# An audio tower on one core: the first layer norm's two products as fp32r pairs, the experts a round later, new orders

## What is computed

```python
# tok: a window of 8 positions, weights filt * W
out = jnp.einsum('blfd,fd,fdk->blk', windows, filt, W)
h = jax.nn.relu(out + b_k)
# attention on layernorm(h), one head, softmax over the positions of one sequence
h = h + attn(layernorm(h))
# experts on layernorm(h): 8 of them, hidden width 128, the two best by gate with softmax weights
h1 = jax.nn.relu(jnp.einsum('td,edh->teh', x_flat, W1) + b1)
y = jnp.einsum('teh,ehd->ted', h1, W2) + b2
h = h + jnp.einsum('ted,te->td', y, combine)
```

## Time and profile before

| | us |
|---|---|
| median of 3 runs | 298.57 (297.52 to 299.38) |
| profiled execution, its own time | 298.85 |
| its span | 297.1 |
| PE busy | 279.3 (94%) |
| DVE busy | 241.1 (81%) |
| ACT busy | 238.9 (80%) |
| POOL busy | 103.8 (35%) |

### The profile page before, as it was taken

One profiled execution on the slowest core, in us unless ns is written; L12 is line 12 of the kernel. 1 busy time (PEld: TensorE's weight loads), 2 busy tenths in 40 slices (PEclk: granted clock), 3 DMA queues, 4 the chain that ended last, 5 costly groups with the idle time before them and its releaser, 6 DMA issues.

```text
span 297.1 us, 6188 instructions
## 1 busy us (share of the span) xinstructions
PE 279.3 (94%) x1737; PEld 200.4 (67%) x1737; DVE 241.1 (81%) x890; ACT 238.9 (80%) x549; POOL 103.8 (35%) x99
## 2 busy tenths in 40 slices
PE   7776999999999999999999999999998999998993
PEld 6544657777777768677777777686776675665572
DVE  2576669989897979889898979798898899895666
ACT  3449598898998889898989989898887788876762
POOL 2204023442536162443415351715342151506051
PEclk9998899999999999999999999999999999999999
DMA  6430206061433526170624426250605133242301
GB/s 189 108 96 9 73 34 176 4 172 57 114 113 76 152 71 158 37 191 4 164 65 109 118 71 159 71 155 31 163 2 130 45 104 89 87 105 69 91 19 34
DMA packets 12785, 27.58 MB, mean 93 GB/s; under 512 B 3152, under 2 KB 5456, under 8 KB 12752
## 3 DMA queue, kind: packets, MB, share of 16 engines
q1 hardware_dynamic: 12464, 26.91, 33.8%
q10 hardware_dynamic: 288, 0.28, 0.3%
HBM read 20.85 MB, written 2.27 MB: 78 GB/s over the span
## 4 chain that ended last, share of the span: by engine, by line
PE 69%; DVE 12%; DMA 7%; issue 5%; ACT 4%; POOL 1%; POOLq 0%; SPq 0%; DVEq 0%; ACTq 0%
PE bank_y L1379 15%; PE bank_a L1290 11%; PE bank_h L1363 7%; PE bank_h L1364 7%; PE bank_s L1307 5%; PE bank_s L1419 4%; DMA kk<-kk 4%; PE bank_s L1318 4%; PE bank_s L1386 3%; DVE acc L820 3%; PE bank_b L1390 2%; PE bank_s L1390 2%; PE bank_s L1440 2%; PE bank_b L1386 2%; PE bank_b L1430 1%
## 5 line engine op out<-in xcount | busy, mean ns | idle before, releaser
L465 ACT ACTIVATE hid<-bank_h,col 128x496 f32<-128x496 f32 x128 | 84.3, 672 | 10.8 <-PE bank_h L1364 7.1
L374 POOL TENSOR_TENSOR p<-p,rmask 124x496 f32<-124x496 f32 x32 | 32.5, 1016 | 97.9 <-DVE rmask L863 97.7
L1379 PE MATMUL bank_y<-hid,w_sb 128*64 128x248 f32 x508 | 63.7, 380 | 0.8 <-DVE acc L820 0.7
L1363 PE MATMUL bank_h<-xs,w_hi 128*128 128x496 f32 x128 | 58.1, 454 | 0.2 <-DVE xs L256 0.2
L820 DVE SCALAR_TENSOR_TENSOR acc<-bank_y,col,cb 128x248 f32<-128x248 f32 x127 | 53.1, 468 | 4.7 <-PE bank_y L1379 1.9
L1364 PE MATMUL bank_h<-xs,w_lo 128*128 128x496 f32 x128 | 49.5, 387 | 0.0
L1379 PEld LDWEIGHTS bank_y<-hid,w_sb 128*64 128x64 f32 x508 | 32.8, 136 | 24.7 <-issue 11.2
L268 POOL TENSOR_TENSOR total<-acc 128x496 f32<-128x496 f32 x16 | 20.0, 1251 | 46.1 <-DVE acc L820 45.9
L456 ACT ACTIVATE p<-bank_s,nmax 124x248 f32<-124x248 f32 x64 | 29.3, 464 | 2.3 <-DVE nmax L852 1.1
L388 POOL TENSOR_TENSOR x_lo<-x,x_hi 128x512 fp32r<-128x512 f32 x16 | 20.6, 1291 | 24.9 <-ACT x_hi L524 24.9
L1363 PEld LDWEIGHTS bank_h<-xs,w_hi 128*128 128x128 f32 x128 | 24.1, 189 | 7.0 <-issue 3.6
(11 more groups left out here) (120 smaller groups left out, 545.8 us busy)
## 6 DMA issues: line engine op xcount, KB each, us to landing
cb<-weights SPq DMA_DIRECT2D x60, 248.0 KB, 3.9
kk<-kk SPq DMA_DIRECT2D x16, 248.0 KB, 3.0
x<-xt SPq DMA_DIRECT2D x15, 256.0 KB, 3.5
out<-h SPq DMA_DIRECT2D x16, 124.0 KB, 3.7
w_sb<-w SPq DMA_DIRECT2D x3, 256.0 KB, 4.0
wtok_sb<-wtok SPq DMA_DIRECT2D x1, 256.0 KB, 2.7
x<-xt ACTq DMA_DIRECT2D x1, 256.0 KB, 3.8
weights<-ct_sb SPq DMA_DIRECT2D x15, 15.5 KB, 1.4
```

Of the source, the lines that this page charges most:

```text
L374: pool.tensor_tensor(p_sb[b][0:HALF, :, :], p_sb[b][0:HALF, :, :], rmask[0:HALF, b, :].unsqueeze(2).to_broadcast([HALF, 2, WIN]), ALU.mult ...
L465: act.activation(hid[2 * (p % 2) + s][:, :], bank_h[s][:, 0:TOK], ACT.Relu, bias=col[:, C_B1 + e:C_B1 + e + 1]).then_inc(hid_ready[s], 1)
L1363: pe.matmul(bank_h[e % 2][:, 0:TOK], w1_hi[:, e, :], xs[m % 2][:, :], start=True, stop=False)
L1379: last = pe.matmul(dst[b * D:b * D + D, :], w2_sb[:, 2 * p + s, :], hid[2 * (p % 2) + s][:, b * WIN:(b + 1) * WIN], start=True, stop=True)
```

## The change

- **Products.** From group 3 (`SPLIT_FROM`, the fourth) on, the first centring and the first variance are two fp32r products each, of a high and a low part, in place of one fp32 product. Their matrices are cast once into `center_r` and `mean_r` (DVE, in `expert_low`).
- **Parts.** ACT's `rectify` writes the high part of h, by a Relu with an fp32r result. POOL gets four instructions a group: h in full (`full_h`), its low part (`low_h`), the high part of the squares (`high_square`), their low part (`low_square`).
- **Experts.** They lag one round more behind the rest of the group, with eight `hid` buffers for four. The loop runs for t = 4 to 11.
- **Orders.** All the order functions of all engines are written anew.

```diff
-        hid = [sb(f"hid{i}", [128, TOK]) for i in range(4)]
+        hid = [sb(f"hid{i}", [128, TOK]) for i in range(EXPERTS)]
...
-        LOOP_FROM, LOOP_TO = 3, 13
+        LOOP_FROM, LOOP_TO = 4, 12
+        SPLIT_FROM = 3
...
+            def full_h(d):
+                pool.wait_ge(hsum_ready, d + 1)
+                pool.wait_ge(h2_ready, d - 1)
+                pool.tensor_scalar(h[d % 2][:, :], hsum[:, :], 0.0, None, ALU.max).then_inc(h_ready, 1)
+
+            def low_h(d):
+                pool.wait_ge(h_ready, d + 1)
+                pool.wait_ge(hh_ready, d - SPLIT_FROM + 1)
+                pool.wait_ge(cen[0], d)
+                pool.tensor_tensor(h_lo[:, :], h[d % 2][:, :], h_hi[:, :].bitcast(F32),
+                                   ALU.subtract).then_inc(hl_ready, 1)
+
+            def high_square(d):
+                pool.wait_ge(sqr[0], d + 1)
+                pool.wait_ge(var[0], d)
+                pool.tensor_copy(s_hi[:, :], sq[0][:, :]).then_inc(sh_ready, 1)
+
+            def low_square(d):
+                pool.wait_ge(sh_ready, d - SPLIT_FROM + 1)
+                pool.tensor_tensor(s_lo[:, :], sq[0][:, :], s_hi[:, :].bitcast(F32),
+                                   ALU.subtract).then_inc(sl_ready, 1)
...
-                after(act, y_done, 4 * m + p - 1)
-                act.activation(hid[2 * (p % 2) + s][:, :], bank_h[s][:, 0:TOK], ACT.Relu,
+                after(act, y_done, 4 * m + p - 3)
+                act.activation(hid[e][:, :], bank_h[s][:, 0:TOK], ACT.Relu,
...
             def square(g, which, src):
                 act.wait_ge(cen[which], g + 1)
-                after(act, var[which], g)
+                if which == 0 and g > SPLIT_FROM:
+                    act.wait_ge(sl_ready, g - SPLIT_FROM)
+                else:
+                    after(act, var[which], g)
...
+                    act.wait_ge(cen[0], d)
+                    act.activation(h_hi[:, :], hsum[:, :], ACT.Relu).then_inc(hh_ready, 1)
...
             def expert_low():
+                dve.wait_ge(par_const, 16)
+                dve.tensor_copy(center_r[:, :], center).then_inc(set_norm, 1)
+                dve.tensor_copy(mean_r[:, :], meanof).then_inc(set_norm, 1)
...
             def fill():
+                expert_high()
                 both_taps(0)
                 attention_parameters()
...
             def variance(g, which, dst):
+                if which == 0 and g >= SPLIT_FROM:
+                    pe.wait_ge(sl_ready, g - SPLIT_FROM + 1)
+                    pe.matmul(dst[:, WIN:2 * WIN], mean_r[:, :], s_hi[:, :], start=True, stop=False)
+                    pe.matmul(dst[:, WIN:2 * WIN], mean_r[:, :], s_lo[:, :], start=False,
+                              stop=True).then_inc(var[0], 1)
+                    return
...
+                pe.wait_ge(set_norm, 2)
+                pe.wait_ge(hl_ready, c - SPLIT_FROM + 1)
+                pe.matmul(bank_b[:, 0:WIN], center_r[:, :], h_hi[:, :], start=True, stop=False)
+                pe.matmul(bank_b[:, 0:WIN], center_r[:, :], h_lo[:, :], start=False, stop=True).then_inc(cen[0], 1)
```

More of the change, by code:

```diff
@@ L1217, in drain @@
[L1217 to L1232 removed]
+                difference(14)
@@ L1504, in fill @@
+                variance(2, 0, bank_b)
+                scores(1, 1)
                 conv(3, range(8, 10))
+                turn_p(1, 0)
+                turn_p(1, 1)
                 conv(3, range(10, 12))
                 turn_weights(0)
-            def iteration(t):
-                a, d, c, n, m = t + 1, t, t - 1, t - 2, t - 3
+                attend(1)
+                queries_keys(2)
+                values(2)
+                second_centre(1)
+                hidden(0, 0)
+                conv(4, range(0, 2))
@@ new lines, in fill @@
+                variance(1, 1, bank_s[0])
+                conv(4, range(2, 4))
+                conv(4, range(4, 6))
+                hidden(0, 1)
+                conv(4, range(6, 8))
+                first_centre(3)
+                gate(1)
+                hidden(0, 2)
+                hidden(0, 3)
+                scores(2, 0)
+                scores(2, 1)
+                hidden(0, 4)
+                conv(4, range(8, 10))
+                hidden(0, 5)
+                variance(3, 0, bank_b)
@@ L1586, in drain @@
+                hidden(11, 3)
+                scores(13, 0)
+                scores(13, 1)
+                conv(15, range(8, 10))
+                hidden(11, 4)
+                conv(15, range(10, 12))
+                hidden(11, 5)
+                variance(14, 0, bank_b)
+                expert_out(11, 0)
                 expert_out(11, 1)
-                conv(15, range(2, 4))
-                gate(12)
-                hidden(11, 5)
-                conv(15, range(4, 6))
                 hidden(11, 6)
-                scores(13, 0)
@@ L1609, in drain @@
+                expert_out(11, 2)
                 attend(13)
+                turn_weights(12)
+                expert_out(11, 3)
                 queries_keys(14)
                 second_centre(13)
+                hidden(12, 0)
+                hidden(12, 1)
+                variance(13, 1, bank_s[0])
+                values(14)
+                hidden(12, 2)
+                first_centre(15)
+                gate(13)
                 hidden(12, 3)
-                values(14)
-                variance(13, 1, bank_s[0])
+                scores(14, 0)
@@ L1635, in drain @@
-                attend(14)
-                queries_keys(15)
-                second_centre(14)
-                values(15)
-                hidden(13, 4)
-                variance(14, 1, bank_s[0])
-                hidden(13, 5)
+                scores(15, 0)
+                hidden(13, 4)
+                scores(15, 1)
+                hidden(13, 5)
+                hidden(13, 6)
+                expert_out(13, 0)
                 expert_out(13, 1)
-                hidden(13, 6)
-                gate(14)
```

982 lines of the change are left out of this document (597 added, 385 removed).

## The result

The changed kernel takes **301.25 us** (median of 6 runs, 300.71 to 303.31) against 298.36 for the kernel before (6 runs, 297.42 to 299.38): a ratio of 1.0115, 95% interval 1.009 to 1.0141. It is slower by about 1%, where I had forecast a gain: 294.8, with 0.12 for slower by over 1% and 0.36 for a change within 1%. The time lies inside my range of 288 to 301.5, at its end. The profiled execution of the changed kernel took 303.31 with a span of 301.5 and is the slowest of its six; the spans of the others are 298.9 to 300.0. So some 2 us of what its trace shows at the clock are more than typical.

What follows compares the result with a forecast made beforehand. PE was taken to set the loop's pace, with no engine full in the drain. Loop -3.9, fill -1.15, drain -0.8 and POOL's holds +2.1 gave -3.75 against 298.85, so 295.1, as median 294.8 us; 8-in-10 range 288 to 301.5.

Steps and rivals of the forecast that it cites:

- -3.9 forecast: Loop, group 1 to 11: ten turns of 15.94 us instead of 16.33, PE still setting the pace.
- The two savings of 0.19: PE, each group from 3 on: first centring and first variance each cost 0.23 instead of 0.42 us.
- the fill, -1.15 forecast: Start to group 1's second centring: the later start of hsum and the gains of the new order sum to -1.15 us.
- term for the cast, +1.9: Fill: the early cast of w1 waits for its loads, so DVE reaches hsum at 11.4 instead of 9.58.
- The other terms, -1.1, -1.8, -0.6 and +0.45: Fill: convolution pair moved behind -1.1, expert outputs a round later -1.8, index search moved -0.6, values before second centring +0.45.
- so it takes them in: Tail: 23.1 us for about 12 of PE work absorbs the later experts' 2.6 us, so 0 counted.
- the split's terms there: Drain and tail: half of PE's savings counted, -0.8; POOL's added instructions holding DVE, +2.1.
- the +1.3 that I had for drain and tail: Group 11 to the end: -0.8 from PE's savings and +2.1 from POOL's holds of DVE, together +1.3 us.
- My sign of being wrong: Drain: the forecast is wrong above all if the 16.17 us between groups moves by more than 0.5 either way.
- The fourth rival: Loop and drain: POOL's instructions hold DVE until it sets the pace past 0.76 us a group; 299.8 to 307.1, chance 0.15.
- Rivals 1 to 3: Drain gains, 288.0, chance 0.17; loop turn stays 16.3, 298.7, chance 0.17; fill only longer, 297.9, chance 0.08.
- rival 1: Drain: new order lets it run at DVE's 14.7 us a group, four groups saving 5.9; 288.0 us, chance 0.17.

Runs made afterwards that it cites:

- e3: Changed kernel with the split undone (single fp32 products, POOL's four instructions gone), new orders and later experts kept: 307.10 us.
- e1: Changed kernel with only the cast of w1 moved back behind the low keys of group 0: 298.29 us.
- e11: Changed kernel with POOL waiting for the early cast of w1 before the low inputs of group 1: 300.01 us.
- e2: Changed kernel with 16 dummy products in PE's idle stretch between the convolutions of groups 0 and 1, cast still early: 299.85 us.
- e5: e1 with 22 dummy products on PE in two waits of the fill, around the first turns of groups 0 and 1: 295.68 us.
- e10: Kernel before with 10 dummy products on PE in the wait for group 0's scaled scores: 297.15 us.
- e7: Kernel before with POOL's four instructions added at e4's places, writing to tiles nobody reads, products left fp32: 309.10 us.
- e6: e5 with two first expert layers of group 0 in place of the dummies around group 1's turn: 295.64 us.
- e12: e5 with 16 more products, the high product of each first expert layer of groups 14 and 15 done twice: 298.26 us.
- e13: Kernel before with 16 more products, the high product of each first expert layer of groups 14 and 15 done twice: 301.10 us.
- e14: e5 with the split for groups 3 to 11 only, single fp32 products again for 12 to 15: 296.17 us.
- e4: Kernel before with only the split, for groups 4 to 15, in the old orders and without the experts' lag: 311.73 us.
- e9: Kernel before without the 16 products with the low part of w1 for groups 14 and 15: 296.78 us.
- e8: e1 without the 16 products with the low part of w1 for groups 14 and 15: 297.36 us.

## Why the prediction was wrong

**Loop: right in the turn, too many turns.** -3.9 forecast; the turn came to 15.89 for 15.94. The two savings of 0.19 are there. Two things I had not counted cancel: a stall of 0.17 ahead of the scores (DVE's `mask`, held by POOL in e3) that went too, and 0.14 that the new orders cost (e3). The ten turns gave -2.1 in the profiled run and -2.7 in e1, since the last two already follow the drain's orders and are longer.

**The failed step: the fill, -1.15 forecast, +5.4 in the profiled run.** Its term for the cast, +1.9, cost 3.0 us of the program's time (e1 against the changed kernel). The wait for the load was sized rightly (10.7). Missing were the hold of 1.0 by POOL's instruction beside the cast (e11: 1.2 us of the time), which I had looked for in the loop and the drain only, and PE's clock, which falls in an idle time of 4.1 us and stays low behind it (e2: 1.4). The three overlap: 1.9, 1.2 and 1.4 are more than the 3.0 they cost together, for e11's edit raises the clock too, and e1's fill loses to the clock in other places. The other terms, -1.1, -1.8, -0.6 and +0.45, sum to -3.05. At full clock they gave -0.7 at most (e5 against e10; -0.2 against e7), and with the clock that this order gets, +1.2 (e1 against before). I had counted the expert outputs that leave the fill as time won. They stood mostly in waits, and the work there had kept PE's clock up, so far as the runs tell (e6 shows it for two first layers): e1 has 0.66 in 40 to 50 us, and 2.6 us came back when dummies stood there and in the gap before.

The Trainium skill (TensorE: Matmul & The Clock Gate, "Part 1: The HAM clock gate") gives the two levels that these windows show and says that activity releases the lower one; the windows of e1 and e5 agree. It puts the penalty of the ramp at under 1% of a typical kernel's span. The falls here are others, in the middle of the fill, and no ramp of the start: e5 against e1 is 0.9% and e2 against the changed kernel 0.5%.

**The second failed step: "so it takes them in", 0 for the tail.** I set 23.1 us against "about 12" of PE work and so forgot the four `spread_last`, 3.7 us by their rows; 15.5 before and 18.1 after is right. The tail grew by 4.2 and the drain shrank by 3.1, because the last groups' experts moved from one to the other; together +1.1, or nearer 2 against a typical before. At the second centring of group 11 the changed kernel has three expert layers and two outputs more still to do than before, 3 x 0.45 + 2 x 0.91 = 3.2 us that the fill no longer does. Work added near the end cost 0.7 to 0.8 of itself (e12, e13), so by my estimate that is +2.4; no run takes this work out of the end to show it. That the split's terms there were 0.8 gained and 2.1 lost, 1.3 lost in all, is not borne out either: e14 gives 0.5 gained at most. So the +1.3 that I had for drain and tail came near the measured +1.1 to +2 by luck, for other reasons than mine. My sign of being wrong did come true: the drain's distance moved from 16.17 to 15.4.

**The fourth rival** (0.15) ends near where the time ended, but not by its mechanism: in the changed kernel DVE's busy time in a turn rose by 0.13 us. Its rule was off in one point as well. I took DVE's idle time in a turn, 0.76 us beyond the attention product's wait, for slack; what counts is the way from the attention product over `lg` to the scores, and there the old kernel has none (PE already waits 0.1 us: `lg` ends at 148.89, the scores start at 149.03). e4 and e7 show that the mechanism was there for the taking, 1.1 us a turn, and that the new orders and the lag, which by themselves cost, are what keeps it off: 13.4 us more with the split in the old orders, 5.85 less with it in the new. The rows point to the places of the instructions: `kmask`, `mask` and the last sum take 0.36, 0.16 and 0.41 us in the changed kernel, 0.82, 0.64 and 0.83 in e7. What the round of slack adds was not tried. Rivals 1 to 3 did not occur as told; the drain alone came half way to rival 1.

**Open:** why two runs of one kernel differ in the fill's clock (the changed kernel's six spans go with clocks of 0.967 to 0.983). Not every low stretch costs time: e12's profiled run, with e5's fill, had the lower level from 17.8 to 21.2 us and was at group 1 after 44.0 us, e5's after 44.2.

## What to carry to other kernels

Price a moved instruction on every engine that touches it: who runs beside it, and how long the engine behind it then idles, since TensorE's idle time can be paid twice, once as the wait and once in its clock. Work that stands in waits of the fill is free and keeps the clock (e6). Moved to the end, it costs most of its length where the engine is full (0.7 to 0.8 in e12 and e13), and nothing where another chain sets the pace: putting two layers back gained nothing in e6. And a part of a change that loses alone may be what lets another part gain: here e5, the changed kernel with the cast back and 22 dummy products, is with e6 the best version, 295.68 us, 1.0% (0.7 to 1.2) under the kernel before; 0.9 us of that, less surely measured, the kernel before can have from dummies alone (e10).

## What the runs showed of the hardware

- 22 dummy products in two waits of some 2.5 us each took 2.6 us off the program (e5); 16 in a wait of 4.1 us took 1.4 off (e2).
- Leaving out and adding the same 3.7 us of PE's work in the tail did not mirror each other: -1.4 and +3.0 us on the kernel before (e9, e13). In e8 the granted clock also fell, to 0.78, behind the gap.
- A 128x1024 cast on DVE took 1.69 us beside a POOL subtraction of 1.26 and 0.69 alone, and a 124x4 operation up to 1.09 for 0.16; a 124x264 one that reads PSUM took 0.41 beside POOL, as without it.
- A product's record overstates it: 0.39 us long, 0.23 from start to start.
